# Attention scores from two 12-bit parts in two halves of the array's rows, in place of three bfloat16 parts in four column strips

## What is computed

```
h = _layernorm(x, axis=-1) * (1 + ca) + sa            # x: 8 batches, 512 tokens, 128 features
q = (h @ Wq.T).reshape(B, S, NH, DK)                  # 16 heads of 8 features
k = h @ Wk.T                                          # one key head of 8 features
v = h @ Wv.T                                          # one value head of 8 features
dist = softmax(einsum('bhqd,bkd->bhqk', q, k) / sqrt(8), axis=-1)
att = einsum('bhqk,bkd->bhqd', dist, v)
x = x + ga * att
```

## Time and profile before

| | us |
|---|---|
| median of 3 runs | 621.04 (618.94 to 621.79) |
| span of the profiled execution, first to last instruction | 616.6 |
| PE busy | 554.9 (90%) |
| DVE busy | 496.7 (81%) |
| ACT busy | 443.5 (72%) |
| POOL busy | 320.6 (52%) |

### The profile page before, as it was taken

One profiled execution on the slowest core, in us unless ns is written; L12 is line 12 of the kernel. 1 busy time (PEld: TensorE's weight loads), 2 busy tenths in 40 slices (PEclk: granted clock), 3 DMA queues, 4 the chain that ended last, 5 costly groups with the idle time before them and its releaser, 6 DMA issues.

```text
span 616.6 us, 18921 instructions
## 1 busy us (share of the span) xinstructions
PE 554.9 (90%) x6699; PEld 307.3 (50%) x6699; DVE 496.7 (81%) x1134; ACT 443.5 (72%) x776; POOL 320.6 (52%) x574
## 2 busy tenths in 40 slices
PE   3669999999999999999999999999799999899970
PEld 2222334333443443443343343343289998799970
DVE  5887999898789779789789779888667777656687
ACT  5683588888788778778877877878765555367771
POOL 1623010134456656666667566666326757665670
PEclk9989999999999999999999999999899999899995
DMA  6299400310311220220220140001223223232645
GB/s 190 66 282 343 132 10 10 75 37 8 78 30 29 69 58 21 70 65 18 61 79 16 35 105 17 27 20 29 51 62 95 79 79 100 84 90 65 201 138 175
DMA packets 49868, 49.32 MB, mean 80 GB/s; under 512 B 15616, under 2 KB 44336, under 8 KB 49056
## 3 DMA queue, kind: packets, MB, share of 16 engines
q1 hardware_dynamic: 42256, 36.89, 21.8%
q0 software_dynamic: 4320, 9.38, 4.7%
q10 hardware_dynamic: 3200, 1.84, 1.0%
HBM read 29.40 MB, written 17.10 MB: 75 GB/s over the span
## 4 chain that ended last, share of the span: by engine, by line
PE 66%; DVE 17%; ACT 5%; issue 3%; DMA 3%; POOL 2%; SPq 2%; DVEq 0%; ACTq 0%; POOLq 0%
PE ps L1096 15%; PE ps L1055 14%; PE ps L1086 12%; DVE neg_max L1401 10%; PE ps L1164 10%; PE ps L1175 9%; ACT P L1263 3%; ACT diag L1273 2%; PE ps L1123 1%; DMA k_parts<-parts 1%; PE ps L1138 1%; PE ps L1155 1%; PE ps L1074 1%; POOL h_sorted L810 1%; PE ps L1130 1%
## 5 line engine op out<-in xcount | busy, mean ns | idle before, releaser
L1401 DVE TENSOR_REDUCE neg_max<-ps 128x1 f32<-128x512 f32 x512 | 321.1, 684 | 54.5 <-PE ps L1055 52.2
L1263 ACT ACTIVATE P<-ps,zero 128x1024 f32<-128x1024 f32 x256 | 272.0, 1110 | 72.8 <-PE ps L1086 71.0
L1055 PE MATMUL ps<-K,Q 128*32 128x512 bf16 x2048 | 183.3, 383 | 5.5 <-DVE neg_max L1401 5.1
L1086 PE MATMUL ps<-Q,K 128*32 128x512 bf16 x2048 | 155.9, 381 | 5.5 <-ACT P L1263 5.1
L1096 PE MATMUL ps<-P,V 128*32 128x512 f32 x1024 | 134.1, 598 | 1.2 <-ACT P L1263 1.1
L1055 PEld LDWEIGHTS ps<-K,Q 128*32 128x32 bf16 x2048 | 54.5, 96 | 109.3 <-DVE neg_max L1401 59.8
L1613 POOL DMA_INDIRECT y_rows<-P,to_now x71 | 73.9, 1041 | 62.9 <-DVE P L1453 30.7
L1319 ACT ACTIVATE parts<-ps,parts 128x128 f32<-128x128 f32 x228 | 64.9, 370 | 41.8 <-PE ps L1164 39.5
L1086 PEld LDWEIGHTS ps<-Q,K 128*32 128x32 bf16 x2048 | 52.3, 97 | 75.7 <-issue 29.5
L810 POOL DMA_INDIRECT h_sorted<-diag,slot x64 | 64.7, 1010 | 28.6 <-POOL max_parts L79 13.4
L1164 PE MATMUL ps<-parts 128*128 128x128 f32 x456 | 61.6, 279 | 2.7 <-DVE parts L1441 1.3
(11 more groups left out here) (239 smaller groups left out, 576.5 us busy)
## 6 DMA issues: line engine op xcount, KB each, us to landing
Q<-q_parts SPq DMA_DIRECT2D x24, 384.0 KB
xs<-h_sorted SPq DMA_DIRECT2D x71, 72.0 KB
W<-w_t SPq DMA_DIRECT2D x2, 2048.0 KB, 11.2
q_parts<-parts SPq DMA_DIRECT2D x8, 384.0 KB, 3.5
Q<-y_rows SPq DMA_DIRECT2D x6, 512.0 KB, 4.5
diag<-att_u SPq DMA_DIRECT2D x128, 16.0 KB
Q<-max_parts SPq DMA_DIRECT2D x96, 4.0 KB, 1.9
out<-Q SPq DMA_DIRECT2D x6, 256.0 KB, 2.3
```

Source lines behind the costliest of these rows:

```text
L1055: ins = eng.matmul(ring_bank(*unit)[QUAD * q:QUAD * (q + 1), :], Q[buffer_of(g)][:, g % NG * G + j, at:at + QUAD], K[buffer_of(g)][:, 0, : ...
L1086: ins = eng.matmul(bank(2 * u + j)[QUAD * q:QUAD * (q + 1), :], K[p][:, 1, at:at + QUAD], Q[p][:, g % NG * G + 2 * u + j, :], start=True, ...
L1263: nc.scalar.activation(P[s % 2][:, 2 * u:2 * u + 2, :], bank(2 * u, 2).rearrange("p (j t) -> p j t", j=2), ACT.Exp, bias=zero[:], scale=SC ...
L1401: eng.tensor_reduce(neg_max[g % 2][:, j * T + s:j * T + s + 1], ring_bank("maximum", g, s, j), AX.X, ALU.max, negate=True).then_inc(ring_u ...
```

## The change

Queries and keys are split in two parts, not three: one rounding to the type float32r and one subtraction (`split_in_two`; in the preparation a cast on ACT and a subtraction on DVE per operand). The parts are stored as 4-byte words. The 16 heads are laid in two halves of the array's rows, even heads in rows 0 to 63 and odd ones in rows 64 to 127, so Q has half as many head slots; a half uses 4 x 8 product rows and 2 rows for the two parts of the maximum. A bank is one matmul of 64 rows and 128 columns. Both maxima of a pair of heads are issued together, in the two halves, then both scores. The intermediate `rest` and the `mid` step are gone. Clearing Q on ACT and loading rows of ones are replaced by small memsets on POOL. All 8 batches have their own part buffers (partly in W1 and W2, which are therefore loaded after all stores have landed). The loads of a batch are 13 DMAs, not 10, and a shift is 4, not 3. The tail's buffers move, its work does not.

```diff
-def split_in_three(own, whole, rest, part):
-    own.link(own.eng.tensor_copy(part[0], whole))
-    own.link(own.eng.tensor_tensor(rest, whole, part[0], ALU.subtract))
-    own.link(own.eng.tensor_copy(part[1], rest))
-    own.link(own.eng.tensor_tensor(part[2], rest, part[1], ALU.subtract))
+def split_in_two(own, whole, part):
+    own.link(own.eng.tensor_copy(rounded(part[0]), whole))
+    own.link(own.eng.tensor_tensor(rounded(part[1]), whole, part[0], ALU.subtract))
...
+            for r in halves:
+                for i in (0, 1):
+                    at = HALF * r + 2 * DK * i
+                    eng.dma_start(Q[p][at:at + 2 * DK, :, :].rearrange("p h t -> p (h t)"),
+                                  q_parts[b, i, r].rearrange("d h t -> d (h t)")[:, None, :].to_broadcast([DK, 2, NH // 2 * S])
                                   ).then_inc(loaded[p], 16)
+                    for n in (0, 1):
+                        eng.dma_start(K[p][at:at + 2 * DK, n, :].rearrange("p (q t) -> p q t", q=T),
...
-            for operand in (rw, K[0], K[1]):
-                eng.memset(operand[:].bitcast(I32), 0).then_inc(op_set, 1)
+            own = Chain(eng, op_set)
+            own.link(eng.memset(rw[:].bitcast(I32), 0))
+            for p in (0, 1):
+                for r in (0, 1):
+                    for n in (0, 1):
+                        own.link(eng.memset(K[p][shift_place(r), n, :], float(n)))
+                    own.link(eng.memset(Q[p][shift_place(r), :, :], 0.0))
             eng.wait_ge(mod_out, START + 1)
...
+            for b in range(B):
+                eng.wait_ge(stored[b], START + STORES)
             eng.dma_start(W1[:, :, 0:F], w1_t).then_inc(experts_loaded, 16)
...
                     unit = ("maximum", g, s, j)
                     wait_free(eng, *unit)
-                    for q in range(128 // QUAD):
-                        at = 128 * s + QUAD * q
-                        ins = eng.matmul(ring_bank(*unit)[QUAD * q:QUAD * (q + 1), :], Q[buffer_of(g)][:, g % NG * G + j, at:at + QUAD],
-                                         K[buffer_of(g)][:, 0, :], start=True, stop=True, tile_position=(0, QUAD * q))
-                    ins.then_inc(ring_full, 1)
+                    p, r = buffer_of(g), j % 2
+                    eng.matmul(ring_bank(*unit), operand(Q[p], r)[:, g % NG * 2 + j // 2, 128 * s:128 * (s + 1)], operand(K[p], r)[:, 0, :],
+                               start=True, stop=True, tile_position=(HALF * r, 0)).then_inc(ring_full, 1)
...
+                    for r in (1, 0):
+                        ins = eng.matmul(bank(2 * u + r), operand(K[p], r)[:, 1, 128 * s:128 * (s + 1)], operand(Q[p], r)[:, g % NG * 2 + u, :],
+                                         start=True, stop=True, tile_position=(HALF * r, 0))
                     ins.then_inc(score_done, 1)
...
-                            if g + 2 < GROUPS:
+                            if g + 2 < GROUPS and j % 2 == 0:
                                 maximum(g + 2, s, j)
+                                maximum(g + 2, s, j + 1)
                             if j % 2 == 0:
                                 scores(g, s, j // 2)
```

More of the change, by code:

```diff
@@ L7 @@
 FP32 = mybir.dt.float32
-BF16 = mybir.dt.bfloat16
+F32R = mybir.dt.float32r
 I32 = mybir.dt.int32
@@ L337, in prepare_gpsimd @@
                                   ALU.mult).then_inc(diag_done, 1)
-        def quarters_of(operand, quarters):
-            words = operand[:].bitcast(FP32).rearrange("p h t -> p (h t)")
-            return [words[:, n * NH * S // 8:(n + 1) * NH * S // 8] for n in quarters]
         def prepare_scalar(eng):
-            def clear(p, quarters):
-                for part in quarters_of(Q[p], quarters):
-                    nc.scalar.activation(part, zero[:].to_broadcast(list(part.shape)), ACT.Copy).then_inc(cleared, 1)
             def deviations(tiles):
@@ L557, in adaln_block @@
         CD = 4
-        y = [carved(Q[p // 2], in_Q, 2048 * (p % 2), T, 2, D) for p in range(CD)]
-        first = [carved(Q[p // 2], in_Q, 2048 * (p % 2) + 1024, T, D) for p in range(CD)]
-        res = [carved(Q[p // 2], in_Q, 2048 * (p % 2) + 1536, T, D) for p in range(CD)]
+        y = [carved(Q[p // 2], in_Q, 1024 * (p % 2), T, 2, D) for p in range(CD)]
+        first = [carved(diag, in_diag, 512 * p, T, D) for p in range(CD)]
+        res = [carved(diag, in_diag, 512 * (CD + p), T, D) for p in range(CD)]
         RING = 3
@@ L941, in shift @@
                 def shift(g):
-                    eng.wait_ge(max_split, START + (g + 1) * 4)
-                    for blk in range(3):
-                        at = QUAD * blk + 24
-                        eng.dma_start(Q[buffer_of(g)][at:at + 1, heads_of(g), :], max_parts[g % 2][:, blk, :]).then_inc(shift_loaded[g % 2], 16)
+                    if g == 0:
+                        eng.wait_ge(op_set, START + SET_ROWS)
+                    eng.wait_ge(max_split, START + (g + 1) * 2)
+                    for r in (0, 1):
+                        for part in (0, 1):
+                            at = HALF * r + PRODUCTS + part
+                            eng.dma_start(Q[buffer_of(g)][at:at + 1, pairs_of(g), :], max_parts[g % 2][8 * r:8 * r + 8, part, :]
+                                          ).then_inc(shift_loaded[g % 2], 16)
                 def regroup(g):
@@ L1002, in _ @@
                 shift(0)
-                for k in range(SETS):
-                    eng.wait_ge(stored[k], START + tiles_at(k, SETS, B) * STORES)
-                eng.wait_ge(cleared, START + 8)
-                load_operands(eng, 1, 1, batch_loaded, 0, 3)
+                load_operands(eng, 1, 1, batch_loaded)
                 eng.wait_ge(row_out, START + B)
@@ L1600, in split @@
                 def split(g):
-                    own = Chain(eng, max_split, g * 4, passed)
+                    own = Chain(eng, max_split, g * 2, passed)
                     wait_taken(eng, "maxima turned", g)
                     if g >= 2:
-                        eng.wait_ge(shift_loaded[g % 2], START + g // 2 * 48)
+                        eng.wait_ge(shift_loaded[g % 2], START + g // 2 * 64)
                     eng.sem_inc(passed, 1)
-                    split_in_three(own, neg_max_T[g % 2][:], max_rest[g % 2][:], [max_parts[g % 2][:, part, :] for part in range(3)])
+                    split_in_two(own, neg_max_T[g % 2][:], [max_parts[g % 2][:, part, :] for part in range(2)])
                 def scatter(t):
@@ L1675 @@
            L0_c, L0_wmod):
-    import ml_dtypes
     import numpy as np
```

158 lines of the change are left out of this document (65 added, 93 removed).

## The result

The changed kernel took 835.95 us (828.7 to 836.05, 4 runs) where the kernel before took 619.99 (618.81 to 621.79, 4 runs): a ratio of 1.345, 95% interval 1.339 to 1.351. The forecast was 614.4, the range 596 to 642.

What follows compares the result with a forecast made beforehand. It took PE's maxima to bound the loop, DVE close behind and SP's shift just in time. 616.6 + 6 (late start) - 9.6 (refill batches) - 3 (first and last groups) = 610.0, plus 4.4 around it: 614.4 us, range 596 to 642.

Steps and rivals of the forecast that it cites:

- the part on the matmuls: PE's maxima and scores: a pair of banks takes 0.22 to 0.3 us, so 64 pairs a batch need 17 us, not 28.
- the clock falls in the refill's wait: Rival: PE waits some 3 us for the shift six times, its clock halves, 12 us in all, 626; chance 0.15.
- the three: The rivals: one half after the other (653), the clock falls in the refill's wait (626), DVE and ACT pace every group (596).
- Halves at once: Matmuls in PE's two row halves run together, 0.22 to 0.3 us a pair, with float32r not worked like float32.
- one half after the other: Rival: a pair takes 0.43 us, PE stays as busy and pays the tiling changes, 653 us; chance 0.18.
- Changes of tiling, 0.11 each, two a strip, hidden: PE switching tiling around values: 32 times a batch, 3.5 us a batch, hidden while PE has 11 us to spare.
- The order: Both maxima before the scores ties scores to DVE's pace, a pair each 1.22 us; costs nothing while DVE paces.
- A group of 11.2 where the shift is in time: Loop groups without a refill: 9.8 us of maxima, 0.3 of statistics and reciprocals, 1.1 of remaining idle time.
- The refill's SP queue, 13.5: Refill group: extra loads and a shift DMA add 2.3 us ahead of the shift; the group takes 13.5 us, not 12.2.
- Some 15 us or more in six waits: Sign for the forecast: scores' wait for max_parts' DMAs, 1.1 us before, grows to some 15 us or more.
- Preparation, 6 us late: Ahead of the loop: POOL's memsets, then weights queued before the shift, start the loop 6 us late; bounds 2 early, 12 late.
- A clock row under 1.00 in each refill group: Listed as a sign that the forecast is wrong: the granted clock drops below full in every group with a refill.

Runs made afterwards that it cites:

- e10: e1 again, timed in rounds: the changed kernel with all 64 rows of each half driven and Q and K cleared whole; 681.42 us, ratio 1.044.
- e12: e9 with each of DVE's maxima taken over the first 256 of 512 keys only; 615.16 us, ratio 0.993.
- e14: e12 again, in rounds against the kernel before on another chip; 641.45 us, ratio 0.987.
- e18: The kernel of e12 and e14 once more, profiled on a chip where the kernel before took 646.49 us; 640.0 us.
- e2: The changed kernel, 34 rows kept, with maxima and scores reading only the upper 16 bits of each word as bfloat16; 816.72 us.
- e1: The changed kernel with all 64 rows of each half driven, Q and K cleared whole in 6 memsets; 669.94 us, ratio 1.032.
- e5: e10 with the order of before on TensorE: one maximum, both scores, one maximum; 670.14 us, ratio 1.026.
- e9: e6 with the experts' weights loaded behind the shift of group 1 and e5's order; 641.17 us, ratio 1.033.
- e6: e10 with Q cleared on ACT in quarters, as before the change, and K still on POOL; 672.32 us, ratio 1.033.
- e3: The kernel before, bfloat16 in four column strips, with only the first 32 of 128 rows in maxima and scores; 963.87 us.

## Why the prediction was wrong

The step that failed is in the part on the matmuls: "PE then needs some 17 us for the 64 pairs of a batch where it needed 28, and is no longer the bound". It priced every matmul at the full clock, because rows of before had it at 1.00. With 34 rows in each half the clock is at 0.50 most of the loop, a pair takes 0.43 us and not 0.23 and the values 1.87 and not 0.87, and a batch takes 73 to 75 us (301.37 to 376.48 from one refill to the next) and not 47.1. Driving 64 rows, with Q and K cleared whole for it, brings the ratio from 1.345 to 1.044 (e10). The rival "the clock falls in the refill's wait" named the clock, but by another mechanism, six idle waits, and priced it at 12 us. In the changed kernel the case that came was none of the three; falls of the clock behind such waits showed up in e12, e14 and e18, once the rows were right.

Point by point:

- *Halves at once.* Right. Two maxima start within 0.01 us of each other (321.25 x2), and at full clock inner pairs follow each other by 0.23 us; the first pair behind another form takes 0.34, which is not among the prediction's terms. float32r went in one pass (e2). The rival "one half after the other" is refuted.
- *Changes of tiling, 0.11 each, two a strip, hidden.* Size and count right, but not hidden. At the full clock the values take 1.00 and not 0.88 up to the next row-half matmul, and a pair takes 0.33 and not 0.22 up to the values: 0.12 and 0.11. "TensorEngine Tiling (Array Packing)", Key Properties, in the Trainium skill has a change of mode drain the engine; the trace agrees. With the first pair's weight loads (0.11) and the wait of a lone maximum for the ring they take back most of what fewer matmuls save. "PE's busy share well under 80%" did not come even near the full clock: 86% of the span in e1, 94% in a stretch of its loop.
- *The order.* The ring of three was counted against PE's long stretches, not against pairs that want two free banks at once. Undoing it won 11 us at 64 rows (e5).
- *A group of 11.2 where the shift is in time.* Not reached: 12.4 a group in e9 (398.1 / 32), against 12.0 before.
- *The refill's SP queue, 13.5.* Right in mechanism, but it can't be seen in the changed kernel, whose groups of 18 us hide it, nor at 64 rows (about 1 us). "Some 15 us or more in six waits" came, as 10 to 13 in 7 or 8, in the kernels with the shortest groups, 11.9 to 12.1 us on average (e12, e14, e18), against 11.8 in the forecast.
- *Preparation, 6 us late.* Right in mechanism, too small. The memsets end at 25.66 (predicted 24.8), the modulation starts at 26.07 (25.2), the first copy at 30.34 (29.5). The period of a batch was 2.83 us (30.34 to 50.12, seven periods), not 2.3, which gives 4 of the 12 us that the first scores came later than forecast (84.11, predicted 72). The other 8 were not separated. The weights were issued at 63.43 (58) and the shift at 69.43, in 6.91 us, behind them. TensorE worked from 52 to 84 us at a clock of 0.53.
- *What would show it.* "A clock row under 1.00 in each refill group" stood in the list as a sign against; it was the loudest row of the page, and not in refill groups alone.

POOL's memsets did one thing that was not foreseen. Rows of POOL, then of DVE, in the changed kernel:

```profile
7.89 3.51 POOL L325 MEMSET Q<- 2x4096 f32 x1
11.45 1.10 POOL L324 MEMSET K<- 2x512 f32 x2
12.61 3.51 POOL L325 MEMSET Q<- 2x4096 f32 x1
```

```profile
8.44 2.98 DVE L411 TENSOR_SCALAR silu_den<-silu_den 128x8 f32<-128x8 f32 x1
11.46 0.20 DVE L412 RECIPROCAL silu_den<-silu_den 128x8 f32<-128x8 f32 x1
11.70 0.17 DVE L413 TENSOR_TENSOR siluT<-silu_den,cT 128x8 f32<-128x8 f32 x1
...
13.03 3.11 DVE L175 TENSOR_SCALAR ln_rstd<-ln_rstd 128x8 f32<-128x8 f32 x1
```

A tensor_scalar of 8 elements, 0.17 us before the change, ends when the memset of Q beside it ends (8.44 + 2.98 = 11.42, and 7.89 + 3.51 = 11.40), twice; reciprocal and tensor_tensor beside a memset take what they always did. A third tensor_scalar, at 12.43 beside the last 0.12 us of a memset of K, was not held. "SBUF — State Buffer", SBUF: two separate sides, in the Trainium skill says that VectorE in its two-port modes and GpSimd hold a shared pair of ports one at a time, for a whole instruction, and that VectorE work with two inputs contends only with a GpSimd instruction that reads SBUF, which a memset does not. The two long rows and the tensor_tensor agree with it; the third tensor_scalar is too short a case to tell. In the changed kernel this hid behind POOL's own lateness. In e1, with 9.6 us less of memsets, the modulation began at 20.42 instead of 14.48, behind the tensor_scalar that ended at 16.17; but POOL's scales, behind the memsets themselves, ended only at 18.98, so both had a part. e6 removed both (15.06).

## What to carry to other kernels

Before a matmul is cut to fewer rows, ask what it does to the granted clock, not only to the count of instructions: here 2048 matmuls of all 128 rows became 512 of 34, two at once, for the maxima as for the scores, and the loop took half as long again; filling the rows up won back 22% of the time (1.345 to 1.044). Look at the clock of the stretch first, and price PE's steps at a clock that the new form has been seen to get. And when an engine is halved, count what its neighbour allows: with DVE at 0.61 us a maximum and the old strip at 2.6 us, there were some 0.16 us a strip to win (4 x 0.61 against 2.6), with a DMA queue and its effect on the clock just behind them.

## What the hardware showed that was not expected

- The granted clock went with the number of rows at a PE busy share of 93 to 100%: 0.50 to 0.53 with 32 of 128 rows in column strips (e3, 100 to 600 us), 0.55 to 0.60 with 34 of 64 in two halves (100 to 600 us), long stretches of both levels with 48 (0.64 to 1.00), 0.91 to 1.00 with 64 (e1, e9, e10, e12 and e18, 100 to 400 us), where the kernel before has 1.00. Added rows whose products are all zero count. Why, and what decides at 48, stays open, as does the low clock of e9 ahead of its loop with 64 rows (0.51, where e12 had 1.00).
- A change between row halves and column strips cost 0.11 to 0.12 us at the full clock, and a float32r weight load of 128 columns took 0.18 us where a bfloat16 one took 0.10; where it is not hidden, the pair behind it takes 0.34 and not 0.24 us.
- A memset on POOL of 4096 elements took 3.51 us on 2 partitions (the changed kernel) and 3.52 on 128 (e1).
- Chips differ by 4 to 5% on the same kernel (620 and 646 to 652 us), most of it behind the attention (168 and 187 us).
